# Capped experts of a two-layer block: own buffers for each expert, five gathers ahead of the first scatter, outputs signalled tile by tile

## The chip, the cores and the metric

The kernel runs on one core of a Trainium2 chip. The metric is the device time of one execution in microseconds (us), lower is better. The kernel before was timed three times: 1220.89, 1223.37 and 1225.88 us, a median of 1223.37 us.

## The reference

16 sequences of 256 tokens with 128 channels pass through two layers, each an attention and a feed-forward part, each wrapped as x + layernorm(part(...)). The first feed-forward part is a gated mixture, the second attention is a power attention. Only the last part is touched here, a mixture with capped experts (8 experts, the last of which passes its tokens through; 7 real ones, 512 tokens each, hidden width 512):

```python
cap = math.ceil(n_tok / n_exp * CAPACITY_FACTOR)               # 4096 / 8 = 512
weights_flat = softmax(x @ router_w.T + router_b)               # top 2 kept, the rest zero
sorted_indices = jnp.argsort(-expert_mask, axis=0)[:cap]        # first 512 tokens of each expert
inputs = x_flat[used_idx] * sorted_mask                         # gather
h = jax.nn.relu(jnp.einsum('ceh,ehi->cei', inputs, experts_inter))
out = jnp.einsum('cei,eih->ceh', h, experts_out) * in_w[..., None]
combined = jnp.zeros_like(x_flat).at[used_idx].add(out)         # scatter
combined = combined + x_flat * (noop_w * noop_mask)[:, None]
# then: x + layernorm(combined)
```

## The kernel before, in words

The three earlier parts (`soft_layers`, `gated_layer`, `power_layer`) and the routing (`route`) fill the span up to about 1107 us. `route` leaves in on-chip memory the row numbers for each expert's gather and scatter (`idx_in`, `idx_out`, 28 columns of 128 rows: 7 experts of 4 tiles) and in HBM the table `tokens` (all tokens, with their two weights beside the 128 channels).

Then comes `capped_mixture` (L2336 on), a program of its own on each engine, tied by semaphores. For each expert e of 7:

- GpSimd (POOL) issues `gather(e)`, four indirect DMAs (L2411) of 128 rows each from `tokens` into `xe`, and `scatter(e)`, four indirect DMAs (L2418) of 128 rows each from `res` into the HBM tensor `expert_outputs`. Only GpSimd issues these, one after the other. `gather(e)` for e of 3 and more waits until the buffer of expert e-3 is free (`s_turn`, `s_two`), `scatter(e)` until VectorE has scaled that expert's outputs (`s_res`). The loop at the end of the GpSimd program sets the order.
- TensorE (PE) transposes the four tiles (`turn`, L2446), multiplies by the first weight in 4 matmuls (`up`, L2454) and by the second in 16 (`down`, L2463). Its order is up(e), turn(e+1), down(e-1). An fp32 matmul stands in the trace as two records.
- ScalarE (ACT) evicts the transposes (L2509) and applies relu (L2514).
- VectorE (DVE) forms the slot weights from the gathered rows (`slot_weights`, L2546 and L2549), scales the four output tiles into `res` (`scale`, L2557) and multiplies five tiles of the tokens by the pass-through weight (`pass_through`, L2563).

`xe` has three buffers, `res`, `slot_w`, `xT` and `hid` two. The output tiles of one expert share one of two PSUM banks, by e % 2.

When all 28 scatters have landed (`s_sent`), SyncE (SP) loads `expert_outputs` back in 16 DMAs (L2393, `got`). TensorE adds per block of four tiles the pass-through rows (`passed`, L2485) and the two loaded halves (`gathered`, L2491); the first four blocks' `passed` come before the wait for `s_sent`, the other four behind it. VectorE, ScalarE and GpSimd normalise and add the residual (L2581, L2521, L2529, L2425), and SyncE stores each block.

Of the kernel before, what the change touches and what calls it, by code (L numbers as in the profile page):

```python
# [30 lines left out]
F32 = mybir.dt.float32  # L31
# [4 lines left out]
ALU = mybir.AluOpType  # L36
# [2299 lines left out]
def capped_mixture(nc, region, idx_in, idx_out, pick, noop, xe, Y, X, cst, cstb, wi, wo, out, yd, od):  # L2336

    NX, TB, FC = NE - 1, CAP // P, F1 // P  # L2340
    NBLK = NTILE // TB
    with ExitStack() as ctx:  # L2342
        take = semaphores(nc, ctx)
# [6 lines left out]

        xT = sb("xT", [P, 2, CAP])
        hid = sb("hid", [P, 2, FC, CAP])
        res = sb("res", [P, 2, TB, D])
        got = sb("got", [P, 2, NTILE, D])
        stats = sb("stats", [P, NTILE, 6])
        mv = sb("mv", [P, NTILE, 2])
        rs = sb("rs", [P, NTILE])
        nm = sb("nm", [P, NTILE])
        two = sb("two", [P, TB, 2])
        slot_w = sb("slot_w", [P, 2, TB])  # L2360
        lv = sb("lv", [P, TB])
        eps = sb("eps", [P, 1])
        ps = ctx.enter_context(nc.psum_tensor("cps", [P, 8, 512], F32))
        turn_ps, hid_ps, out_ps = ps[:, 0:2, :], ps[:, 2:6, :], ps[:, 6:8, :]
        s_ready = sem("s_ready")
        s_xe = [sem(f"s_xe{k}") for k in range(3)]
# [6 lines left out]
        s_sent = [sem(f"s_sent{k}") for k in range(2)]  # L2373
        s_got = [sem(f"s_got{k}") for k in range(NBLK)]
        s_pass = sem("s_pass")
        s_two = sem("s_two")
# [8 lines left out]

        @block.sync
        def _(sp):
            sp.wait_ge(s_sent[0], 16 * TB * 4)
            sp.wait_ge(s_sent[1], 16 * TB * 3)
# [12 lines left out]
        def _(pool):  # L2402
            pool.memset(eps[:], EPS_LN).then_inc(s_ready, 1)

            def gather(e):
                if e >= 3:
                    pool.wait_ge(s_turn, e - 2)
                    pool.wait_ge(s_two, 2 * (e - 3) + 1)
                for c in range(TB):
                    t = e * TB + c  # L2410
                    pool.indirect_dma_start(xe[:, e % 3, c, :], None, yd,  # L2411
                                            bass.IndirectOffsetOnAxis(ap=idx_in[:, t:t + 1], axis=0)).then_inc(s_xe[e % 3], 16)

            def scatter(e):
                pool.wait_ge(s_res, e + 1)
                for c in range(TB):
                    t = e * TB + c
                    pool.indirect_dma_start(od, bass.IndirectOffsetOnAxis(ap=idx_out[:, t:t + 1], axis=0),  # L2418
                                            res[:, e % 2, c, :], None)\
                        .then_inc(s_sent[e % 2], 16)  # L2420

            def residual(n):
                pool.wait_ge(s_f, n + 1)
                part = slice(TB * n, TB * n + TB)
# [12 lines left out]
        @block.tensor  # L2437
        def _(pe):
            ident = cst[:, C_IDENT:C_IDENT + P]

            def turn(e):
                pe.wait_ge(s_xe[e % 3], 16 * TB * (e // 3 + 1))
                if e >= 2:
                    pe.wait_ge(s_xT, e - 1)
                for c in range(TB):
                    last = pe.transpose(turn_ps[:, e % 2, c * P:(c + 1) * P], xe[:, e % 3, c, 0:D], ident)  # L2446
                last.then_inc(s_turn, 1)

            def up(e):
                pe.wait_ge(s_xT, e + 1)  # L2450
                for c in range(FC):
                    if e >= 1:
                        pe.wait_ge(s_hid, FC * (e - 1) + c + 1)
                    pe.matmul(hid_ps[:, c, :], wi[:, e, c * P:(c + 1) * P], xT[:, e % 2, :], start=True, stop=True)\  # L2454
                      .then_inc(s_hp, 1)

            def down(e):
                pe.wait_ge(s_hid, FC * (e + 1))
                if e >= 2:
                    pe.wait_ge(s_res, e - 1)  # L2460
                for t in range(TB):
                    for c in range(FC):
                        last = pe.matmul(out_ps[:, e % 2, t * D:(t + 1) * D], hid[:, e % 2, c, t * P:(t + 1) * P],  # L2463
                                         wo[:, e, c, :], start=(c == 0), stop=(c == FC - 1))
                last.then_inc(s_op, 1)
# [12 lines left out]

            def passed(n):
                if 2 <= n < 6:  # L2480
                    pe.wait_ge(s_hid, FC * (NX - 1) + n - 1)
                if n >= 6:
                    pe.wait_ge(s_res, NX - 1 if n % 2 != (NX - 1) % 2 else NX)
# [12 lines left out]
            for n in range(NBLK):  # L2496
                if n == NBLK // 2:
                    pe.wait_ge(s_sent[0], 16 * TB * 4)
                passed(n)
            for n in range(NBLK):  # L2500
                gathered(n)

        @block.scalar
        def _(act):
            for e in range(NX):
# [4 lines left out]
                for c in range(FC):  # L2510
                    act.wait_ge(s_hp, FC * e + c + 1)
                    if e >= 2:
                        act.wait_ge(s_op, e - 1)
# [26 lines left out]
        @block.vector  # L2540
        def _(dve):
            def slot_weights(e):
                dve.wait_ge(s_xe[e % 3], 16 * TB * (e // 3 + 1))
                if e >= 1:
                    dve.wait_ge(s_two, 2 * e)
                dve.tensor_tensor(two[:], xe[:, e % 3, :, D:D + 2], pick[:, TB * e:TB * e + TB, :], ALU.mult)\  # L2546
                   .then_inc(s_two, 1)
                dve.wait_ge(s_two, 2 * e + 1)
                dve.tensor_reduce(slot_w[:, e % 2, :], two[:], AX.X, ALU.add).then_inc(s_two, 1)  # L2549

            def scale(e):
                dve.wait_ge(s_op, e + 1)
                dve.wait_ge(s_two, 2 * e + 2)
                if e >= 2:
                    dve.wait_ge(s_sent[e % 2], 16 * TB * (e // 2))
                for c in range(TB):
                    last = dve.tensor_scalar(res[:, e % 2, c, :], out_ps[:, e % 2, c * D:(c + 1) * D],  # L2557
                                             slot_w[:, e % 2, c:c + 1], None, ALU.mult)
                last.then_inc(s_res, 1)

            def pass_through(e):
                for t in range(5 * e, min(NTILE, 5 * e + 5)):
# [27 lines left out]
def build(nc, dram, out):  # L2590
    with ExitStack() as ctx:
# [151 lines left out]
```

## Time and profile before

| | us |
|---|---|
| median of three runs | 1223.37 (1220.89 to 1225.88) |
| the profiled execution's own time | 1220.48 |
| its span | 1218.7 |
| mean granted TensorE clock in it | 0.969 of full speed |
| GpSimd busy in the span | 663.2 (54%) |
| TensorE busy in the span | 1113.3 (91%) |

The span is the time from the first to the last recorded instruction; 1.78 us of the execution's own time lie around it. The clock is given as a share of full speed (2.4 GHz): 1.00 is 2.4 GHz and 0.50 is 1.2 GHz. In a timeline row, the bracket at the end is the idle time of the engine before that row and what ended it; "issue" there means that the engine waited for nothing that the profile shows. A gather or scatter on GpSimd counts as busy while GpSimd issues it; the data land later.

### The profile page before, as it was taken

To read this page: it belongs to the slowest core of one execution; us is meant where nothing else is said; L and a number is where in the kernel's file an instruction comes from. 1 tells how busy PE (TensorE), PEld (TensorE's weight loads), DVE (VectorE), ACT (ScalarE), POOL (GpSimd) and SP (SyncE) were. 2 spreads that over 40 slices of the span, in tenths; PEclk is the share of its full clock that TensorE was granted. 3 is DMA by queue.
4 is the path that set the end of the run, shared out by engine and by line. 5 is a ranking of instruction groups with operands and counts; after the bars stand their busy time and mean duration, and the time that the engine had idled before them with its cause. 6 is when DMAs were issued, how large, how long until landed. Compare 5 with 4: busy or idle time off the path is not lost. (4 is left out here: it accounts for less than half of the span.)

```text
span 1218.7 us, 33462 instructions
## 1 busy us (share of the span) xinstructions
PE 1113.3 (91%) x11747; PEld 628.6 (52%) x11747; DVE 994.4 (82%) x2703; ACT 855.1 (70%) x1830; POOL 663.2 (54%) x695
## 2 busy tenths in 40 slices
PE   5999999999999998999999998999999999928976
PEld 2344444444444444666556555555566665524652
DVE  4899999999999896689988899789899999773223
ACT  1688888888888887656555555687899998733314
POOL 3234334554433330556556667577788887734753
PEclk9999999999999998999999999999899999957998
DMA  4111111111111110000000000001112222032117
GB/s 121 32 40 38 41 39 41 41 37 39 42 41 45 37 32 11 2 1 2 1 2 2 2 1 9 22 18 48 41 48 56 57 57 56 21 140 44 50 42 207
DMA packets 83460, 48.91 MB, mean 40 GB/s; under 512 B 17432, under 2 KB 80353, under 8 KB 83297
## 3 DMA queue, kind: packets, MB, share of 16 engines
q1 hardware_dynamic: 80816, 42.62, 13.5%
q0 software_dynamic: 1792, 3.70, 1.1%
q8 instruction: 97, 1.59, 0.6%
q14 instruction: 67, 0.54, 0.1%
q10 hardware_dynamic: 688, 0.46, 0.1%
HBM read 16.52 MB, written 10.26 MB: 22 GB/s over the span
## 5 line engine op out<-in xcount | busy, mean ns | idle before, releaser
L627 DVE TENSOR_REDUCE mxsS<-scoreS 128x2 f32<-128x512 f32 x512 | 328.7, 684 | 38.9 <-PE scoreS L766 33.9
L515 ACT ACTIVATE PTS<-stS 128x512 f32<-128x512 f32 x512 | 283.5, 591 | 53.0 <-PE stS L770 52.8
L2014 POOL TENSOR_TENSOR ghid<-gprod,ghid 128x512 f16<-128x512 f32 x144 | 165.8, 1159 | 139.4 <-ACT ghid L2144 138.2
L766 PE MATMUL scoreS<-QK 31*128 31x256 f16 x1024 | 172.5, 280 | 24.0 <-DVE mxsS L627 11.4
L971 POOL TENSOR_TENSOR PTP<-PTP,EP 128x512 f32<-128x512 f32 x128 | 163.2, 1285 | 50.7 <-ACT PTP L1199 50.6
L770 PE MATMUL stS<-QK 32*128 32x256 f16 x1024 | 168.7, 277 | 1.3 <-ACT PTS L515 1.3
L2144 ACT ACTIVATE ghid<-gprod 128x512 f16<-128x512 f32 x144 | 90.2, 627 | 94.4 <-DVE gprod L2303 93.5
L691 PE MATMUL pvS<-PTS,Vx 128*32 128x256 f32 x2048 | 138.8, 389 | 0.4
L1372 DVE TENSOR_SCALAR AP<-score_psP 128x768 int32<-128x768 int32 x128 | 121.5, 949 | 10.6 <-PE score_psP L1528 10.0
L766 PEld LDWEIGHTS scoreS<-QK 31*128 31x128 f16 x1024 | 53.8, 93 | 145.6 <-DVE mxsS L627 92.5
L1199 ACT ACTIVATE PTP<-AP,epsP 128x768 f32<-128x768 f32 x128 | 119.2, 931 | 6.6 <-DVE AP L1372 5.9
L388 POOL TENSOR_TENSOR rsS<-veS,halfS 128x2 f32<-128x2 f32 (+1 forms) x32 | 28.0, 874 | 172.2 <-DVE veS L595 89.2
L2096 PE MATMUL up_ps<-ghT,split 128*128 128x512 f16 x432 | 116.8, 379 | 3.3 <-DVE gprod L2303 3.3
L2091 PE MATMUL gate_ps<-ghT,split 128*128 128x512 f16 x432 | 116.9, 379 | 2.9 <-ACT gsg L2157 2.8
L2303 DVE TENSOR_TENSOR gprod<-gsg,up_ps 128x512 f32<-128x512 f32 x144 | 96.1, 682 | 23.9 <-ACT gsg L2157 18.1
L2070 PEld LDWEIGHTS down_ps<-split,ghid 128*128 128x128 f16 x1728 | 102.0, 98 | 17.6 <-issue 3.6
L2070 PE MATMUL down_ps<-split,ghid 128*128 128x128 f16 x1728 | 108.2, 219 | 0.0
L2157 ACT ACTIVATE gsg<-gate_ps 128x512 f32<-128x512 f32 x144 | 84.4, 586 | 28.0 <-PE gate_ps L2091 26.6
L1209 ACT ACTIVATE EP<-decay_psP 128x512 f32<-128x512 f32 x128 | 75.6, 591 | 20.3 <-PE decay_psP L1510 19.6
L691 PEld LDWEIGHTS pvS<-PTS,Vx 128*32 128x32 f32 x2048 | 53.8, 110 | 49.4 <-issue 21.8
L2096 PEld LDWEIGHTS up_ps<-ghT,split 128*128 128x128 f16 x432 | 41.4, 98 | 56.7 <-DVE gprod L2303 8.0
L2268 DVE SCALAR_TENSOR_TENSOR gacc<-down_ps,gcomb,gacc 128x128 f32<-128x128 f32 x224 | 62.6, 341 | 0.0
(341 smaller groups left out, 2233.6 us busy)
## 6 DMA issues: line engine op xcount, KB each, us to landing
QK<-HLS SPq DMA_DIRECT2D x384, 32.0 KB, 1.9
QK<-HLP SPq DMA_DIRECT2D x192, 32.0 KB, 1.9
expert_outputs<-tzero SPq DMA_DIRECT2D x8, 512.0 KB
cgot<-expert_outputs SPq DMA_DIRECT2D x16, 256.0 KB, 4.9
tokens<-XB SPq DMA_DIRECT2D x16, 128.0 KB, 3.1
out_dram<-X SPq DMA_DIRECT2D x8, 256.0 KB, 2.3
wi<-L_ffn_experts_inter_dram SPq DMA_DIRECT2D x7, 256.0 KB, 3.1
wo<-n_L_ffn_experts_out_dram SPq DMA_DIRECT2D x7, 256.0 KB, 3.8
```

The lines of the kernel that those rows point to most:

```text
L515: act.activation(PT[:, n % NPT, :], st_ps[:, (NS * t + n) % 3, :], ACT.Exp, scale=SCALE).then_inc(s_exp, 1)
L627: dve.tensor_reduce(mxs[:, u // 4, :, at], score_ps[:, n % 2, :].rearrange("p (c s) -> p c s", c=TC), AX.X, ALU.max).then_inc(s_max, 1)
L691: last = pe.matmul(pv_ps[32 * j:32 * j + 32, q], Vx[:, t % 3, c, 4 * g + j, :], PT[:, (4 * g + (j ^ 2)) % NPT, S * c:S * c + S], start=(c ...
L766: scored = pe.matmul(score_ps[:, k, cols], QK[part, new, g, 0, rows], QK[part, new, g, 1, :], start=True, stop=True)
L770: turned = pe.matmul(st_ps[:, (NS * t + n) % 3, cols], QK[part, old, g, 1, rows], QK[part, old, g, 0, :], start=True, stop=True)
L971: eng.tensor_tensor(w, w, E[:, n % NE, :], ALU.mult).then_inc(s_wd if n % NU in MULT_BY_DVE else s_wp, 1)
L1199: act.activation(PT[:, n % NW, :], A[:, n % NA, :], ACT.Square, bias=eps[:, 0:1]).then_inc(s_sq, 1)
L1372: dve.tensor_scalar(A[:, n % NA, :].bitcast(I32), score_ps[:, n % 2 * WU:n % 2 * WU + WU].bitcast(I32), 0x7FFFFFFF, None, ALU.bitwise_and) ...
L2014: pool.tensor_tensor(hid[:, n // FC % NHID, 1, c, :], prod[:, n % NPROD, :], hid[:, n // FC % NHID, 0, c, :], ALU.subtract).then_inc(s_hid, 1)
L2070: last = pe.matmul(down_ps[:, x % 2, t * D:(t + 1) * D], hid[:, x % NHID, lh, c, t * P:(t + 1) * P], down_w[:, lw, x % EX, c, :], start=(c ...
L2091: last = pe.matmul(gate_ps[:, n % 2, :], gate_w[:, lw, e, cols], hT[:, n // NQ % 2, lh, :], start=(k == 0), stop=(k == 2))
L2096: last = pe.matmul(up_ps[:, n % 3, :], up_w[:, lw, e, cols], hT[:, n // NQ % 2, lh, :], start=(k == 0), stop=(k == 2))
```

## The change

Every expert gets its own buffer for gathered rows (`xe`, 7 instead of 3), for outputs (`res`, 7 instead of 2) and for slot weights; to make room, the last stage may use all on-chip memory behind its start. The gathers then wait for nothing, and each has a semaphore of its own. GpSimd issues five experts' gathers first, then for each expert its scatter and after it, while there are any left, the gather of expert e+5. VectorE signals `s_res` after each tile instead of after each expert, and every single scatter waits for its own tile. TensorE signals `s_op` after each half of an expert's down matmuls. For the last expert the halves lie in different PSUM banks, so that VectorE scales the first while TensorE writes the second; the second half then waits until expert 5's tiles are scaled. For experts 0 to 5 VectorE still waits for both halves. One semaphore counts all scatters.

```diff
-    NX, TB, FC = NE - 1, CAP // P, F1 // P
+    NX, TB, FC, AHEAD = NE - 1, CAP // P, F1 // P, 5
...
-        res = sb("res", [P, 2, TB, D])
+        res = sb("res", [P, NX, TB, D])
...
+        def out_tile(e, t):
+            bank = t // 2 if e == NX - 1 else e % 2
+            return out_ps[:, bank, t * D:(t + 1) * D]
...
             def gather(e):
-                if e >= 3:
-                    pool.wait_ge(s_turn, e - 2)
-                    pool.wait_ge(s_two, 2 * (e - 3) + 1)
...
             def scatter(e):
-                pool.wait_ge(s_res, e + 1)
                 for c in range(TB):
                     t = e * TB + c
+                    pool.wait_ge(s_res, t + 1)
                     pool.indirect_dma_start(od, bass.IndirectOffsetOnAxis(ap=idx_out[:, t:t + 1], axis=0),
-                                            res[:, e % 2, c, :], None)\
-                        .then_inc(s_sent[e % 2], 16)
+                                            res[:, e, c, :], None)\
+                        .then_inc(s_sent, 16)
...
-            gather(0)
-            gather(1)
-            gather(2)
+            for e in range(AHEAD):
+                gather(e)
             for e in range(NX):
-                if e + 3 < NX:
-                    gather(e + 3)
                 scatter(e)
+                if e + AHEAD < NX:
+                    gather(e + AHEAD)
...
             def down(e):
                 pe.wait_ge(s_hid, FC * (e + 1))
...
+                for half in range(2):
+                    if half == 0 and e >= 2:
+                        pe.wait_ge(s_res, TB * (e - 1))
+                    if half == 1 and e == NX - 1:
+                        pe.wait_ge(s_res, TB * e)
+                    for t in range(2 * half, 2 * half + 2):
+                        for c in range(FC):
+                            last = pe.matmul(out_tile(e, t), hid[:, e % 2, c, t * P:(t + 1) * P],
+                                             wo[:, e, c, :], start=(c == 0), stop=(c == FC - 1))
+                    last.then_inc(s_op, 1)
...
             def scale(e):
-                dve.wait_ge(s_op, e + 1)
                 dve.wait_ge(s_two, 2 * e + 2)
-                if e >= 2:
-                    dve.wait_ge(s_sent[e % 2], 16 * TB * (e // 2))
                 for c in range(TB):
...
+                    dve.wait_ge(s_op, 2 * e + 1 + (c // 2 if e == NX - 1 else 1))
+                    dve.tensor_scalar(res[:, e, c, :], out_tile(e, c), slot_w[:, e, c:c + 1], None, ALU.mult)\
+                       .then_inc(s_res, 1)
...
-        xe = region("xe", [P, 3, CAP // P, D + 2], F32)
+        region = Region(nc, region.at, nc.sbuf_usable_end)
+        xe = region("xe", [P, NE - 1, CAP // P, D + 2], F32)
```

On GpSimd, the DMAs of the last stage stood before in this order (`xe` is a gather, `expert_outputs` a scatter, x16 are four experts):

```order
L2411 DMA xe<-tokens,idx_in 128x130 x16
L2418 DMA expert_outputs<-cres,idx_out 8320x128 x4
L2411 DMA xe<-tokens,idx_in 128x130 x4
L2418 DMA expert_outputs<-cres,idx_out 8320x128 x4
L2411 DMA xe<-tokens,idx_in 128x130 x4
L2418 DMA expert_outputs<-cres,idx_out 8320x128 x4
L2411 DMA xe<-tokens,idx_in 128x130 x4
L2418 DMA expert_outputs<-cres,idx_out 8320x128 x16
L2425 TENSOR_TENSOR X<-X,XB 128x512 x8
```

With the change the same 56 DMAs stand on GpSimd in this order:

```order
L2412 DMA xe<-tokens,idx_in 128x130 x20
L2419 DMA expert_outputs<-cres,idx_out 8320x128 x4
L2412 DMA xe<-tokens,idx_in 128x130 x4
L2419 DMA expert_outputs<-cres,idx_out 8320x128 x4
L2412 DMA xe<-tokens,idx_in 128x130 x4
L2419 DMA expert_outputs<-cres,idx_out 8320x128 x20
L2426 TENSOR_TENSOR X<-X,XB 128x512 x8
```

The gather of expert 4 has moved ahead of the first scatter, that of 5 ahead of the second and that of 6 ahead of the third.

On TensorE, the two last experts' down matmuls stood before in this way, with the `passed` matmuls behind them (a semaphore's name in the brackets is that of its first use in the program, and the number is used again: `s_one` is `s_res` here, `s_bias` is `s_hid`, `s_flat` is `s_xT` and `full_MXaS` is `s_pass`):

```order
L2463 MATMUL cps<-wo,chid 128x128 [waits s_one,s_bias]
L2463 MATMUL cps<-wo,chid 128x128 x15
L2463 MATMUL cps<-wo,chid 128x128 [waits s_one,s_bias]
L2463 MATMUL cps<-wo,chid 128x128 x15
L2485 MATMUL cps<-XB,cst 128x512 [waits full_MXaS,s_flat]
```

With the change, at the same place on TensorE (`s_set` is `s_res`, `s_spread` is `s_hid`, `s_one` is `s_xT` and `free_TS` is `s_pass`):

```order
L2466 MATMUL cps<-wo,chid 128x128 [waits s_set,s_spread]
L2466 MATMUL cps<-wo,chid 128x128 x15
L2466 MATMUL cps<-wo,chid 128x128 [waits s_set,s_spread]
L2466 MATMUL cps<-wo,chid 128x128 x7
L2466 MATMUL cps<-wo,chid 128x128 [waits s_set]
L2466 MATMUL cps<-wo,chid 128x128 x7
L2488 MATMUL cps<-XB,cst 128x512 [waits free_TS,s_one]
```

No matmul has moved; the last expert's 16 have one more wait in their middle.

## Rows read from the trace of the kernel before

**Rows 1.** The page: its head, and its share of the last chain by engine.
```profile
span 1218.7 us, 33462 instructions
...
POOL 4%; PE 2%; issue 2%; ACT 1%; DMA 0%; DVE 0%; POOLq 0%
```

**Rows 2.** The chain of waits, its last part: start us, us, what.
```profile
1175.11 1.14 DVE cres L2557 x4
...
1185.42 2.24 DMA expert_outputs<-cres,idx_out
1187.71 5.13 PE cps L2485 x8
1192.84 3.45 PE cps L2491 x8
```

**Rows 3.** Timeline of GpSimd in the last stage: start us, duration, what, idle before.
```profile
1107.88 1.23 POOL L2411 DMA_INDIRECT xe<-tokens,idx_in  x1 [0.70 <-issue]
1109.40 0.95 POOL L2411 DMA_INDIRECT xe<-tokens,idx_in  x1 [0.30 <-issue]
...
1126.90 0.94 POOL L2411 DMA_INDIRECT xe<-tokens,idx_in  x1 [0.30 <-issue]
1130.17 1.00 POOL L2418 DMA_INDIRECT expert_outputs<-cres,idx_out  x1 [2.33 <-DVE cres L2557]
...
1135.31 0.99 POOL L2411 DMA_INDIRECT xe<-tokens,idx_in  x1 [0.30 <-issue]
...
1140.37 1.00 POOL L2418 DMA_INDIRECT expert_outputs<-cres,idx_out  x1 [0.30 <-issue]
...
1145.50 0.99 POOL L2411 DMA_INDIRECT xe<-tokens,idx_in  x1 [0.30 <-issue]
...
1169.50 0.97 POOL L2418 DMA_INDIRECT expert_outputs<-cres,idx_out  x1 [3.86 <-DVE cres L2557]
...
1176.51 0.97 POOL L2418 DMA_INDIRECT expert_outputs<-cres,idx_out  x1 [2.22 <-DVE cres L2557]
...
1181.60 0.97 POOL L2418 DMA_INDIRECT expert_outputs<-cres,idx_out  x1 [0.30 <-issue]
...
1185.42 0.97 POOL L2418 DMA_INDIRECT expert_outputs<-cres,idx_out  x1 [0.30 <-issue]
```

**Rows 4.** Timeline of TensorE's matmuls in the same stage.
```profile
1128.57 3.60 PE L2454 MATMUL cps<-cxT,wi 128*128 128x512 f32 x8
...
1136.01 3.60 PE L2454 MATMUL cps<-cxT,wi 128*128 128x512 f32 x8
1141.69 0.66 PE L2446 MATMUL cps<-cst,xe 128*128 128x128 f32 x4 [2.08 <-DMA xe<-tokens,idx_in]
1142.18 5.37 PE L2463 MATMUL cps<-wo,chid 128*128 128x128 f32 x32
...
1162.20 0.66 PE L2446 MATMUL cps<-cst,xe 128*128 128x128 f32 x4 [2.60 <-DMA xe<-tokens,idx_in]
...
1171.33 7.31 PE L2463 MATMUL cps<-wo,chid 128*128 128x128 f32 x64
1180.34 3.67 PE L2485 MATMUL cps<-XB,cst 128*128 128x512 f32 x8 [1.70 <-DVE XB L2563]
```

**Rows 5.** DMA issues of the last stage: what, count, median us from issue to landing.
```profile
xe<-tokens,idx_in POOLq DMA_INDIRECT x28, 2.5
expert_outputs<-cres,idx_out POOLq DMA_INDIRECT x28, 2.2
```

**Rows 6.** Timeline of VectorE: the pass-through tiles behind expert 5's scaling.
```profile
1176.15 1.06 DVE L2563 TENSOR_SCALAR XB<-XB,noop 128x128 f32<-128x128 f32 x5
```

**Rows 7.** Engines and granted TensorE clock in two stretches of 2 us.
```profile
core 0: us, PE busy (x) PEld busy (x) DVE busy (x) ACT busy (x) POOL busy (x), PEclk, DMA share, GB/s
1144.00:1146.00 2.00, 2.00 (x11) 2.00 (x11) 0.00 (x0) 0.00 (x0) 1.47 (x2) 0.50 0.19 66
...
1188.00:1190.00 2.00, 2.00 (x3) 0.88 (x3) 0.00 (x0) 0.00 (x0) 0.00 (x0) 0.50 0.51 152
```

More of the change, by code:

```diff
@@ L2359, in capped_mixture @@
         two = sb("two", [P, TB, 2])
-        slot_w = sb("slot_w", [P, 2, TB])
+        slot_w = sb("slot_w", [P, NX, TB])
         lv = sb("lv", [P, TB])
@@ L2364, in capped_mixture @@
         turn_ps, hid_ps, out_ps = ps[:, 0:2, :], ps[:, 2:6, :], ps[:, 6:8, :]
+        def out_tile(e, t):
+            bank = t // 2 if e == NX - 1 else e % 2
+            return out_ps[:, bank, t * D:(t + 1) * D]
         s_ready = sem("s_ready")
-        s_xe = [sem(f"s_xe{k}") for k in range(3)]
+        s_xe = [sem(f"s_xe{e}") for e in range(NX)]
         s_turn = sem("s_turn")
@@ L2372, in capped_mixture @@
         s_res = sem("s_res")
-        s_sent = [sem(f"s_sent{k}") for k in range(2)]
+        s_sent = sem("s_sent")
         s_got = [sem(f"s_got{k}") for k in range(NBLK)]
@@ L2387, in _ @@
         def _(sp):
-            sp.wait_ge(s_sent[0], 16 * TB * 4)
-            sp.wait_ge(s_sent[1], 16 * TB * 3)
+            sp.wait_ge(s_sent, 16 * TB * NX)
             rows = od[0:2 * NT, :].rearrange("(c t p) d -> c p t d", c=2, p=P)
@@ L2405, in gather @@
             def gather(e):
-                if e >= 3:
-                    pool.wait_ge(s_turn, e - 2)
-                    pool.wait_ge(s_two, 2 * (e - 3) + 1)
                 for c in range(TB):
                     t = e * TB + c
-                    pool.indirect_dma_start(xe[:, e % 3, c, :], None, yd,
-                                            bass.IndirectOffsetOnAxis(ap=idx_in[:, t:t + 1], axis=0)).then_inc(s_xe[e % 3], 16)
+                    pool.indirect_dma_start(xe[:, e, c, :], None, yd,
+                                            bass.IndirectOffsetOnAxis(ap=idx_in[:, t:t + 1], axis=0)).then_inc(s_xe[e], 16)
             def scatter(e):
-                pool.wait_ge(s_res, e + 1)
                 for c in range(TB):
                     t = e * TB + c
+                    pool.wait_ge(s_res, t + 1)
                     pool.indirect_dma_start(od, bass.IndirectOffsetOnAxis(ap=idx_out[:, t:t + 1], axis=0),
-                                            res[:, e % 2, c, :], None)\
-                        .then_inc(s_sent[e % 2], 16)
+                                            res[:, e, c, :], None)\
+                        .then_inc(s_sent, 16)
             def residual(n):
@@ L2441, in turn @@
             def turn(e):
-                pe.wait_ge(s_xe[e % 3], 16 * TB * (e // 3 + 1))
+                pe.wait_ge(s_xe[e], 16 * TB)
                 if e >= 2:
@@ L2445, in turn @@
                 for c in range(TB):
-                    last = pe.transpose(turn_ps[:, e % 2, c * P:(c + 1) * P], xe[:, e % 3, c, 0:D], ident)
+                    last = pe.transpose(turn_ps[:, e % 2, c * P:(c + 1) * P], xe[:, e, c, 0:D], ident)
                 last.then_inc(s_turn, 1)
@@ L2458, in down @@
                 pe.wait_ge(s_hid, FC * (e + 1))
-                if e >= 2:
[L2460 to L2465, printed above, removed]
+                for half in range(2):
[8 more added lines that the diff above has]
+                    last.then_inc(s_op, 1)
             for _ in range(24):
@@ L2482, in passed @@
                 if n >= 6:
-                    pe.wait_ge(s_res, NX - 1 if n % 2 != (NX - 1) % 2 else NX)
+                    pe.wait_ge(s_res, TB * NX)
                 part = Y[:, TB * n:TB * n + TB, :].rearrange("p t d -> p (t d)")
@@ L2497, in _ @@
                 if n == NBLK // 2:
-                    pe.wait_ge(s_sent[0], 16 * TB * 4)
+                    pe.wait_ge(s_sent, 16 * TB * NX)
                 passed(n)
@@ L2512, in _ @@
                     if e >= 2:
-                        act.wait_ge(s_op, e - 1)
+                        act.wait_ge(s_op, 2 * (e - 1))
                     act.activation(hid[:, e % 2, c, :], hid_ps[:, c, :], ACT.Relu).then_inc(s_hid, 1)
@@ L2542, in slot_weights @@
             def slot_weights(e):
-                dve.wait_ge(s_xe[e % 3], 16 * TB * (e // 3 + 1))
+                dve.wait_ge(s_xe[e], 16 * TB)
                 if e >= 1:
                     dve.wait_ge(s_two, 2 * e)
-                dve.tensor_tensor(two[:], xe[:, e % 3, :, D:D + 2], pick[:, TB * e:TB * e + TB, :], ALU.mult)\
+                dve.tensor_tensor(two[:], xe[:, e, :, D:D + 2], pick[:, TB * e:TB * e + TB, :], ALU.mult)\
                    .then_inc(s_two, 1)
                 dve.wait_ge(s_two, 2 * e + 1)
-                dve.tensor_reduce(slot_w[:, e % 2, :], two[:], AX.X, ALU.add).then_inc(s_two, 1)
+                dve.tensor_reduce(slot_w[:, e, :], two[:], AX.X, ALU.add).then_inc(s_two, 1)
             def scale(e):
-                dve.wait_ge(s_op, e + 1)
                 dve.wait_ge(s_two, 2 * e + 2)
-                if e >= 2:
-                    dve.wait_ge(s_sent[e % 2], 16 * TB * (e // 2))
                 for c in range(TB):
-                    last = dve.tensor_scalar(res[:, e % 2, c, :], out_ps[:, e % 2, c * D:(c + 1) * D],
-                                             slot_w[:, e % 2, c:c + 1], None, ALU.mult)
-                last.then_inc(s_res, 1)
+                    dve.wait_ge(s_op, 2 * e + 1 + (c // 2 if e == NX - 1 else 1))
+                    dve.tensor_scalar(res[:, e, c, :], out_tile(e, c), slot_w[:, e, c:c + 1], None, ALU.mult)\
+                       .then_inc(s_res, 1)
             def pass_through(e):
```

## The prediction, made before the changed kernel was run

> **What bounds the kernel now.** I read the page's head and its last chain first. The span is 1218.7 us, and the chain that ended last names GpSimd before TensorE, with small shares of the whole span [rows 1]. The diff touches only the stage that starts at about 1107 us, so I asked which wait ends last there. The chain of waits, read backwards from the output, goes through the normalisation to the adding matmuls (L2491), to eight passed matmuls (L2485, 5.13 us), and from there at 1187.71 us to the landing of the last scatter, which GpSimd issued at 1185.42 us [rows 2]. Everything behind 1187.69 us hangs on that one scatter: 1218.7 - 1187.7 = 31.0 us of tail. So the question is when GpSimd issues its last scatter.
>
> GpSimd's timeline shows a nearly closed row of DMA issues [rows 3]. A gather costs 0.95 us plus a gap of 0.30: from the second to the sixteenth it is (1126.90 - 1109.40) / 14 = 1.25 us each. A group of four scatters takes 5.13 us (1140.37 to 1145.50) ahead of a gather and 5.09 us (1176.51 to 1181.60) ahead of another scatter; four gathers behind a scatter take 5.06 us (1135.31 to 1140.37). The 56 issues stretch from 1107.88 to 1185.42 us. Three gaps are longer than 0.30 us: 2.33 before the first scatter (expert 0), 3.86 before the one at 1169.50 (expert 4) and 2.22 before the one at 1176.51 (expert 5); expert 6's group begins at 1181.60 without a wait [rows 3]. Beyond the usual 0.30 they hold 2.03 + 3.56 + 1.92 = 7.51 us in which GpSimd waited for VectorE's scaled outputs. That is all that GpSimd loses.
>
> Why it waited is seen on TensorE [rows 4]. An expert takes 7.44 us there when nothing is late (up starts at 1128.57 and at 1136.01). But the transposes of experts 4 and 6 started 2.08 and 2.60 us late for their gathers, and in the down matmuls behind them the clock is at 0.50, 1.2 GHz [rows 7], so that they take 5.37 us; the hot price is 7.31 / 2 = 3.66 us [rows 4]. The gathers were late because each stood behind a scatter that had waited for the outputs of an earlier expert. It is a ring: GpSimd waits for TensorE's outputs, TensorE then for GpSimd's gathers.
>
> **The change part by part.** All sums are made against the profiled execution (span 1218.7, own time 1220.48).
>
> 1. Gathers ahead. Expert 4's four gathers go into the hole before the first scatter. The twenty gathers' last starts at 1126.90 + 4 x 1.25 = 1131.90, the first scatter at 1133.15, where before it was 1130.17: 3.0 us later, and nobody waits for it, since the loads need all 28. From there on, if no output is late: scatter 0 at 1133.15, gather 5 at 1138.28, scatter 1 at 1143.34, gather 6 at 1148.47, scatter 2 at 1153.53, then 5.09 each: 1158.6, 1163.7, 1168.8, and expert 6's at 1173.9. The last of its four starts 3.82 later (1185.42 - 1181.60 [rows 3]): 1177.7. That is 7.7 us before 1185.42.
>
> 2. Are the outputs ready by then? Gathers land 2.5 us after their issue [rows 5]. Expert 4's have landed at 1134.4, before TensorE wants them at about 1139.4; expert 5's at 1144.6, wanted at 1146.9; expert 6's last is issued at 1152.3 and lands at 1154.8, wanted at about 1154.3, so TensorE waits some 0.5 us. Up starts at 1136.01 as before, then at 1143.45, 1150.89 and 1158.8 (expert 6); down of 5 and 6 runs from 1162.3 to 1169.6 (7.31). VectorE needs 1.14 us for four tiles [rows 2]. Outputs against scatters: expert 4 about 1160.2 against 1163.7, expert 5 about 1167.1 against 1168.8, expert 6 about 1170.5 against 1173.9. The narrowest margin is 1.7 us, so GpSimd runs closed to its end. What is late next is GpSimd's own row of 56 issues.
>
> 3. Signals for each tile. GpSimd's scatters now carry 28 waits instead of 7, and the gathers lose theirs. Behind each waiting DMA the whole rest of the row is queued, and behind its end the loads and the tail. The row shows what a satisfied wait costs: the scatter at 1140.37 has one and stands behind a gap of 0.30 like those without, at 1.00 us instead of 0.97 [rows 3]. Below I bound it by 0, above by 0.40: the gap before the first gather, right behind another kind of instruction, is 0.70. I take 0.00 to 0.03 for each of 21, and 0.1 us in all, since the difference of 0.03 is also seen on a gather (0.99 at 1135.31) and so is not the wait's. VectorE's and TensorE's added signals and waits lie beside their engines' idle time.
>
> 4. The last expert in halves. Its second half's wait for expert 5's scaling falls to about 1166.0 + 1.3 = 1167.3, while the first half runs until 1166.0 + 1.8 = 1167.8: hidden by 0.5 us, and if the cover went, it would cost only TensorE time that has 3 us of margin to the scatter. The gain is nothing as well: the outputs are finished before GpSimd can send them.
>
> 5. Own buffers for outputs and slot weights. No wait before ended with a buffer's release (the three long ones ended with the scaling), so they free nothing, except that gathers may run ahead at all. Cost nothing.
>
> 6. The tail. Passed for the first four blocks starts right after the last pass-through tiles, at about 1171, and ends at 1174.7 (3.67 us [rows 4]); TensorE then waits until 1177.7 + 2.3 = 1180.0, 5.3 us, where before it waited 1187.71 - 1184.01 = 3.7 us. Behind the 3.7 us the clock was at 0.50 [rows 7], and eight matmuls took 5.13 instead of 3.67 us. At most all eight run at 1.2 GHz: 2 x 3.67 = 7.3, 2.2 us more than now; at least they take what they take hot, 1.5 less, of which the loads, then the next in line, leave perhaps 0.2. The stretches behind 2.08 and 2.60 us of idle time cost 5.37 - 3.66 = 1.7 each, 0.25 more than the 1.46 here, so I take 0.4 us.
>
> The Trainium skill, page "TensorE: Matmul & The Clock Gate", section "HAM oscillation — how this bites in real kernels", says that a wait for a DMA between two bursts drops the clock, so that the next burst starts cold. The trace agrees: 0.50 after the wait of 3.7 us. By that rule the longer wait of the changed kernel gives a cold start again and term 6 stays within 0 to 2.2 us; a reading of the trace alone gives the same bounds.
>
> Sum: -7.7 + 0.1 + 0.4 = -7.2 us. Span 1211.5, own time 1213.3. The profiled execution lies 2.9 us below the median of the runs shown; carried over, the median becomes 1223.4 - 7.2 = 1216.2, rounded 1216.
>
> **The rivals.**
> A. As above, GpSimd closed: 1216 (chance 0.72).
> B. TensorE falls behind and GpSimd waits again. For it: TensorE still waits 0.5 us for expert 6's gather, and waits of 2 us brought 1.2 GHz. Against: 0.5 us is short, and even two cold downs (3.4 us) leave expert 5's outputs at 1170.5 against 1168.8, 1.7 us lost. Time 1218 (0.10).
> C. The tail gives it back: all eight passed matmuls at 1.2 GHz, 1.8 us more than taken: 1218 (0.10).
> D. Slower: the price of waits on GpSimd. Each scatter's wait costs, in place of nothing, up to the 0.40 us that the gap of 0.70 has over 0.30. 21 x 0.40 = 8.4 us, 8.3 above my term: 1224.5. It decides from 7.3 / 21 = 0.35 us for each on. Against it stands the scatter with a satisfied wait and a gap of 0.30. Chance 0.04, and some of it lies above 0.5% only if a wait costs over 0.6 us.
> E. Nothing comes of it: GpSimd's issues stretch when they run closed beside VectorE. For each of the seven pass-through groups, 1.06 us [rows 6], an issue would be held up: about 6.8 us with the short last one, and 1223. Against it: the scatter at 1176.51 took 0.97 us in the middle of such a group (1176.15 to 1177.21), as did that at 1185.42 with VectorE idle. Chance 0.04, with everything else that could leave the time as it was. The Trainium skill, page "SBUF — State Buffer", section "SBUF: two separate sides", has such a rule: while VectorE runs an instruction that takes both ports, GpSimd cannot write the descriptors of its DMAs. The two rows just named show no trace of it.
>
> **How the numbers follow.** About 0.5% (6.1 us) is what a measurement of this kernel can tell from no change; that line is at 1217.3, only 1.3 us above my forecast, and the three runs of before lie 5 us apart. Of A some seven tenths fall below it, of B and C a third: 0.52 + 0.07, and a little for a larger gain, 0.60. Slower by over 0.5%: 0.03. The rest, 0.37, is within. For the range I take A with 4 us for the runs' own spread, and let it reach over B and C: 1211.5 to 1221.
>
> **What the changed profile would show.** Steps 1 and 2 are right if GpSimd's timeline has no gap above 0.30 us between its first gather and its last scatter, and that scatter starts at 1177 to 1179 us; wrong if a scatter waits for VectorE. TensorE should have no transpose waiting more than 1 us and no down group above 4 us. Step 3 is right if scatters with waits keep 0.97 to 1.00 us and gaps of 0.30. Step 4 is right if the last expert's first scatter doesn't wait. Step 6 shows in the passed matmuls behind the wait: 5.1 us if I neither gain nor lose, 7 for C. The prediction fails if the last scatter comes at 1182 us or later, or if the tail from its landing to the end is over 33 us.

## The result, and the profile after

| | before | with the change |
|---|---|---|
| median, runs on the same chip, us | 1224.84 (20 runs) | 1215.34 (20 runs, 1211.39 to 1222.06) |
| ratio | | 0.9929, 95% interval 0.9913 to 0.9945 |
| profiled execution: own time, span | 1220.48, 1218.7 | 1217.18, 1215.4 |
| W: first gather's start to last scatter's start | 77.54 | 70.11 |
| tail: last scatter's landing to the end | 31.0 | 32.1 |

The timeline of GpSimd in the changed kernel, first gather to last scatter, columns as in [rows 3]:

```profile
1110.92 1.23 POOL L2412 DMA_INDIRECT xe<-tokens,idx_in  x1 [0.70 <-issue]
...
1136.17 1.00 POOL L2419 DMA_INDIRECT expert_outputs<-cres,idx_out  x1 [0.30 <-issue]
...
1140.03 0.97 POOL L2419 DMA_INDIRECT expert_outputs<-cres,idx_out  x1 [0.30 <-DVE cres L2558]
...
1170.68 1.08 POOL L2419 DMA_INDIRECT expert_outputs<-cres,idx_out  x1 [0.30 <-DVE cres L2558]
1172.07 0.97 POOL L2419 DMA_INDIRECT expert_outputs<-cres,idx_out  x1 [0.30 <-DVE cres L2558]
...
1177.21 0.97 POOL L2419 DMA_INDIRECT expert_outputs<-cres,idx_out  x1 [0.30 <-issue]
...
1181.03 0.97 POOL L2419 DMA_INDIRECT expert_outputs<-cres,idx_out  x1 [0.30 <-issue]
```

The gaps of 2.33, 3.86 and 2.22 us of [rows 3] are gone. Where VectorE is still named as the releaser, the gap is the usual 0.30 us, so nothing was waited for. The last scatter starts 70.11 us after the first gather.

TensorE's matmuls in the changed kernel answer to [rows 4]:

```profile
1142.45 0.60 PE L2446 MATMUL cps<-cst,xe 128*128 128x128 f32 x4
1142.89 3.74 PE L2466 MATMUL cps<-wo,chid 128*128 128x128 f32 x32
...
1157.86 0.66 PE L2446 MATMUL cps<-cst,xe 128*128 128x128 f32 x4 [0.36 <-DMA xe<-tokens,idx_in]
1158.36 3.74 PE L2466 MATMUL cps<-wo,chid 128*128 128x128 f32 x32
...
1165.37 7.31 PE L2466 MATMUL cps<-wo,chid 128*128 128x128 f32 x64
1173.86 3.67 PE L2488 MATMUL cps<-XB,cst 128*128 128x512 f32 x8 [1.19 <-DVE XB L2563]
1183.33 5.22 PE L2488 MATMUL cps<-XB,cst 128*128 128x512 f32 x8 [5.80 <-DMA expert_outputs<-cres,idx_out]
```

The transposes of experts 4 and 6 wait 0 and 0.36 us instead of 2.08 and 2.60, and no down group is above 3.74 us. The wait for the scatters has grown from 3.70 to 5.80 us, and the eight matmuls behind it are as cold as before: 5.22 us. The granted clock there, answering to [rows 7]:

```profile
1182.00:1184.00 2.00, 0.68 (x1) 0.50 (x2) 0.00 (x0) 0.00 (x0) 0.00 (x1) 0.50 0.10 33
1184.00:1186.00 2.00, 2.00 (x3) 0.67 (x2) 0.00 (x0) 0.00 (x0) 0.00 (x0) 0.50 0.71 211
```

The chain of waits of the changed kernel ends in another way than [rows 2]:

```profile
1181.03 2.25 DMA expert_outputs<-cres,idx_out
1183.30 0.37 SPq L2397
...
1187.66 6.43 DMA cgot<-expert_outputs
1194.13 2.00 PE cps L2494 x4
1196.15 0.89 DVE cstats L2581 x4
```

It no longer goes through the cold passed matmuls but through SyncE's row of load issues, from 1183.30 on, and the landing of the load issued at 1187.66. With it the fourth block is there, 10.83 us after the scatters have landed.

### The profile page after: what moved, and what is told of

It reads as the page before. It is cut to its first block and busy times, and to the rows that moved or that the text cites. A ratio compares the mean times of both kernels' runs of the same rounds, so it can differ in the third digit from the quotient of the medians.

```text
span 1215.4 us, 33457 instructions
## 1 busy us (share of the span) xinstructions
PE 1111.4 (91%) x11747; PEld 625.7 (51%) x11747; DVE 997.1 (82%) x2703; ACT 855.4 (70%) x1830; POOL 663.5 (55%) x695
## 5 line engine op out<-in xcount | busy, mean ns | idle before, releaser
L627 DVE TENSOR_REDUCE mxsS<-scoreS 128x2 f32<-128x512 f32 x512 | 328.8, 685 | 38.1 <-PE scoreS L766 33.0
L1372 DVE TENSOR_SCALAR AP<-score_psP 128x768 int32<-128x768 int32 x128 | 121.6, 950 | 11.6 <-PE score_psP L1528 10.7
L1209 ACT ACTIVATE EP<-decay_psP 128x512 f32<-128x512 f32 x128 | 75.7, 591 | 21.7 <-PE decay_psP L1510 21.2
```

The lines of the kernel that those rows point to most:

```text
L627: dve.tensor_reduce(mxs[:, u // 4, :, at], score_ps[:, n % 2, :].rearrange("p (c s) -> p c s", c=TC), AX.X, ALU.max).then_inc(s_max, 1)
L1372: dve.tensor_scalar(A[:, n % NA, :].bitcast(I32), score_ps[:, n % 2 * WU:n % 2 * WU + WU].bitcast(I32), 0x7FFFFFFF, None, ALU.bitwise_and) ...
```

## The experiments

The same program doesn't run alike on every chip, and this came to decide what the experiments could show. So the pairs of exact copies come first, then the variants. Each chip was used in one sitting only, so wherever the text says "on chip 2", the traces can't tell the chip from the occasion.

| run | chip | gathers in a row at the start | up 0 to up 3, us | W, us | tail, us | ratio to before there | before's median there |
|---|---|---|---|---|---|---|---|
| before | not noted | 16 | 20.0 | 77.54 | 31.0 | | 1224.8 |
| the change | not noted | 20 | 20.1 | 70.11 | 32.1 | 0.9929 | 1224.8 |
| before2 | 1 | 16 | 19.9 | 77.51 | 31.3 | 1.0009 | 1223.3 |
| after2 | 1 | 20 | 19.9 | 70.02 | 32.6 | 0.9931 | 1223.3 |
| after3 | 12 | 20 | 19.9 | 69.96 | 32.3 | 0.9955 | 1220.9 |
| order_only_c | 12 | 20 | 19.9 | 69.94 | 32.2 | 0.9940 | 1220.9 |
| ahead4 | 2 | 16 | 22.5 | 81.55 | 32.5 | 0.9986 | 1230.0 |
| order_only | 2 | 20 | 28.9 | 83.25 | 31.6 | 1.0003 | 1230.0 |
| warm | 2 | 20 | 29.0 | 81.72 | 31.0 | 0.9967 | 1230.0 |
| ahead7 | 2 | 28 | 38.1 | 85.40 | 31.6 | 1.0006 | 1230.0 |
| ahead4_b | 15 | 16 | 23.3 | 81.70 | 32.3 | 0.9964 | 1230.4 |
| order_only_b | 15 | 20 | 29.3 | 83.52 | 31.1 | 1.0006 | 1230.4 |
| early_queues | 15 | 20 | 29.7 | 82.12 | 31.8 | 0.9983 | 1230.4 |
| fewer | 15 | 24 | 32.2 | 81.45 | 32.1 | | 1230.4 |

W is the difference of two starts in GpSimd's timeline, as in 1181.03 - 1110.92 = 70.11. "Up 0 to up 3" is the time on TensorE from the start of expert 0's up matmuls to that of expert 3's, as in 1139.02 - 1118.88 = 20.1; what it has above 20 us is time lost to the stalls named issue (TensorE stands still although it waits for nothing that the profile shows), with the cold matmuls behind them.

**Exact copies.** No edit.

> The changed kernel once more, word for word, beside its variants' conditions. In the first four experiments every variant showed something that neither trace of before nor of the change has: from the 28th matmul record of the first expert's down group on, TensorE stood still up to 2.6 us before single instructions, named issue, 1 to 15 us in all. Theory S (the stalls in TensorE's supply of instructions belong to the conditions of the run, not to the variants): this trace shows them too, W (first gather's start to last scatter's) is 75 to 85 us instead of 70.1, and the time is at 1226 to 1230 us. Theory V (the variants' own order or layout brings them): this trace shows none, W is 70.1 us and the ratio to the kernel before is 0.993 as measured before.

> The kernel before once more, word for word, under the same conditions as the changed kernel beside it. Theory S: stalls named issue in the first expert's down group here too, W 78 to 90 us instead of 77.5. Theory V: no stalls, W 77.5 us.

Neither copy stalled. Ratio of after2 0.9931 (0.9908 to 0.9954), W 70.02 against 77.51. That looked like theory V, but the kernel before was at 1223.3 us here and at 1230 us on chips 2 and 15, and that is no variant. The last pair was chosen to tell it apart:

> The changed kernel word for word a third time. All eight traces of variants so far (chips 2 and 15, where the kernel before had a median of 1230 us) have TensorE standing still before single instructions in the first expert's down group; the two traces of the changed kernel and the two of before (chip 1 and the first sessions, before at 1223 to 1225 us) have none. Theory S (it goes with the chip or the session): where the kernel before is at about 1230 us again, this kernel stalls too, W 78 to 86 us and 1224 to 1228 us; where before is at 1224 us, no stall, W 70.1 us and 1215 us. Theory V (it goes with the variants): never a stall here.

> The order alone a third time, in the same conditions as the changed kernel beside it. Where no stall occurs: theory of order W 70 to 71 us and the same time as the changed kernel; rival (signals, halves, own output buffers carry part) W 72 us or more. Where the stalls occur: W 82 to 84 us and a time 2 to 4 us above the changed kernel, because the scatters of an expert then start only behind its fourth scaled tile. By theory V this variant stalls even if the changed kernel beside it does not.

On chip 12 (before 1220.9 us) neither stalled. The variant that had stalled on chips 2 and 15 did not stall here, so the stalls don't belong to the variant: theory V is out. Ratios 0.9955 (0.9935 to 0.9976) and 0.9940 (0.9912 to 0.9967), the same.

**The order alone** (order_only, three times):

```diff
-        s_xe = [sem(f"s_xe{k}") for k in range(3)]
+        s_xe = [sem(f"s_xe{k}") for k in range(NX)]
...
             def gather(e):
-                if e >= 3:
-                    pool.wait_ge(s_turn, e - 2)
-                    pool.wait_ge(s_two, 2 * (e - 3) + 1)
...
-            gather(0)
-            gather(1)
-            gather(2)
+            for e in range(5):
+                gather(e)
             for e in range(NX):
-                if e + 3 < NX:
-                    gather(e + 3)
                 scatter(e)
+                if e + 5 < NX:
+                    gather(e + 5)
...
-        xe = region("xe", [P, 3, CAP // P, D + 2], F32)
+        region = Region(nc, region.at, nc.sbuf_usable_end)
+        xe = region("xe", [P, NE - 1, CAP // P, D + 2], F32)
```

> The kernel before with the order alone changed: seven buffers for gathered rows, gathers without waits, five experts' gathers ahead; still two output buffers, one signal for each expert (7 waits on GpSimd's scatters instead of 28) and no halves. Theory: W 70 to 71 us, the same time as the changed kernel within the measurement. Rival 1 (signals, halves or own output buffers carry part of the gain): W 72 us or more, because a scaling waits for the scatters of two experts earlier or a scatter for its fourth tile. Rival 2 (28 waits on GpSimd cost time each): W shorter than with the change, by 21 times the price of a wait; at 0.1 us each 68.0 us.

> The order alone, without the signals for each tile, the halves and the seven output buffers, once more for the same reason. Theory of order: no wait over 0.5 us on GpSimd, W 70 to 71 us, ratio to before 0.993. Rival 1: a scaling waits for older scatters, W 72 us or more. Rival 2 (a wait has a price): W 68 us.

Where nothing stalled, the order, with the seven buffers for gathered rows that it needs, gives the whole gain. GpSimd's row in order_only_c:

```profile
1113.86 1.23 POOL L2408 DMA_INDIRECT xe<-tokens,idx_in  x1 [0.70 <-issue]
...
1183.80 0.97 POOL L2415 DMA_INDIRECT expert_outputs<-cres,idx_out  x1 [0.30 <-issue]
```

69.94 us, against 69.96 for the whole change beside it. The signals for each tile, the halves and the five more output buffers together brought nothing there, and 28 waits cost no more than 7 (0.02 us in all). The order of before with seven gather buffers is in ahead4 alone, on chips with stalls, so the two are not cleanly separated by a run; but in the kernel before no gather on GpSimd stood behind more than its usual gap of 0.30 us, so no gather had waited for a buffer. On chips 2 and 15 W was 83.3 and 83.5 us, 1.5 and 1.4 us more than in the kernels with signals, halves and output buffers there that have five experts ahead too (warm and early_queues below). So where outputs are late these parts are worth something.

**Four ahead** (ahead4, twice; the output buffers, signals and halves of the change stay):

```diff
-    NX, TB, FC, AHEAD = NE - 1, CAP // P, F1 // P, 5
+    NX, TB, FC, AHEAD = NE - 1, CAP // P, F1 // P, 4
```

> The changed kernel with four instead of five experts' gathers ahead of the first scatter: GpSimd's order is then that of the kernel before, while the own buffers, the signals for each tile and the last expert in halves stay. I measure W, the time from the start of GpSimd's first gather to the start of its last scatter (77.5 us before, 70.1 us with the change). Theory (the order of gathers and scatters made the gain): the waits for VectorE come back at the first scatter and at experts 4 and 5, shortened by 0.8 us each time since a scatter may start behind one scaled tile instead of four; W 75 to 77 us, and 5 to 6 us slower than the changed kernel. Rival (signals and buffers made it): W stays at 70 to 72 us and the time within 2 us of the changed kernel.

> Four gathers ahead instead of five, once more, since the first try ran where TensorE's instructions came late (stalls named issue) on a chip that the changed kernel was not timed on. Without such stalls the theory of order expects: GpSimd waits for VectorE again before the first scatter (1.5 us beyond the gap of 0.30), and at experts 4 and 5; W (first gather's start to last scatter's) 75 to 77 us, time 5 to 6 us above the changed kernel, ratio to before 0.998. Rival (signals and buffers): W 70 to 72, ratio 0.993.

Ratios 0.9986 (0.9969 to 1.0002) and 0.9964 (0.9930 to 0.9998). Both ran on chips with stalls, so W (81.6, 81.7) can't be compared with the 75 to 77 expected, and how much the signals would save with four ahead is not measured. But the ring of the prediction, GpSimd waiting for outputs and TensorE then for gathers, is there. TensorE in ahead4:

```profile
1145.72 0.66 PE L2446 MATMUL cps<-cst,xe 128*128 128x128 f32 x4 [1.15 <-DMA xe<-tokens,idx_in]
...
1157.90 1.12 PE L2446 MATMUL cps<-cst,xe 128*128 128x128 f32 x4 [4.51 <-DMA xe<-tokens,idx_in]
...
1168.50 0.27 PE L2446 MATMUL cps<-cst,xe 128*128 128x128 f32 x1 [0.81 <-DMA xe<-tokens,idx_in]
```

TensorE had lost 2.5 us to the stall, and then waits 1.15 + 4.51 + 0.81 = 6.5 us for gathers, since each late output made a scatter late and it the gather behind it. With five or more ahead no transpose waited for a gather on those chips, although the stalls took 9 to 18 us.

**Seven ahead** (the same line with 7), and what the stalls are made of.

> The changed kernel with all seven experts' gathers ahead of the first scatter. Theory (with five ahead GpSimd's 56 issues are closed, and their sum is the bound): the first scatter comes 10.1 us later, W stays 70.1 us within 0.3 us, since every output is ready early, the 0.36 us wait of TensorE for expert 6's gather goes, and nothing is gained in the time. Rival (TensorE's rest of waiting for gathers still costs, or a later first scatter costs): W changes by more than 0.5 us.

W 85.4 us, ratio 1.0006 (0.9989 to 1.0023), on chip 2: my expectation of an unchanged W was missed, for a reason that I had not thought of. TensorE in ahead7:

```profile
1124.62 3.18 PE L2466 MATMUL cps<-wo,chid 128*128 128x128 f32 x27
1128.93 0.35 PE L2466 MATMUL cps<-wo,chid 128*128 128x128 f32 x1 [1.14 <-issue]
1130.33 0.27 PE L2466 MATMUL cps<-wo,chid 128*128 128x128 f32 x1 [1.05 <-issue]
1133.15 0.37 PE L2466 MATMUL cps<-wo,chid 128*128 128x128 f32 x1 [2.56 <-issue]
...
1142.96 1.01 PE L2454 MATMUL cps<-cxT,wi 128*128 128x512 f32 x1 [1.79 <-issue]
1145.06 4.85 PE L2454 MATMUL cps<-cxT,wi 128*128 128x512 f32 x6 [1.09 <-issue]
```

Single matmuls, which in the down group have no wait of their own behind the first, start 1.4 to 2.8 us apart. It ends at 1145 us; GpSimd's 28 gathers in a row end at 1142.5. In all eight traces with stalls, the longer the first row of gathers, the more time is lost: 2.5 and 3.3 us with 16, 8.9 to 9.7 us with 20, 12.2 us with 24 and 18.1 us with 28. Within some 3 us of the row's end this stall is over, in ahead4 and ahead4_b too, where GpSimd then sits idle for 4 us. In six of the eight traces (not in ahead7 and fewer) a smaller one comes later in the stage, 1.2 to 3.2 us of idle time in all. In order_only its largest part lies 4 us and more behind the last gather, which ends at 1166.2, while GpSimd scatters or waits:

```profile
1170.59 0.51 PE L2459 MATMUL cps<-wo,chid 128*128 128x128 f32 x3 [0.47 <-issue]
1172.01 0.27 PE L2459 MATMUL cps<-wo,chid 128*128 128x128 f32 x1 [0.91 <-issue]
1173.41 2.39 PE L2459 MATMUL cps<-wo,chid 128*128 128x128 f32 x20 [1.13 <-issue]
```

So TensorE's instructions come late mostly while GpSimd gathers, on chips 2 and 15, and not on the others. What makes them late no trace shows: that the gathers do it is argued from the time and the length of the large stall, and the small ones don't fit it everywhere.

**TensorE kept busy in the tail** (warm):

```diff
                 if n == NBLK // 2:
+                    pe.wait_ge(s_res, TB * NX)
+                    for _ in range(20):
+                        pe.matmul(ps[:, 7, :], cstb[:, 0:P], cstb[:, P:2 * P].unsqueeze(1).to_broadcast([P, 4, P]),
+                                  start=True, stop=True)
                     pe.wait_ge(s_sent, 16 * TB * NX)
```

> The changed kernel with 20 added bf16 matmuls of 512 columns into a PSUM bank that is overwritten later, placed on TensorE between the fourth and the fifth block's passed matmuls, ahead of its wait for the scatters (they compute nothing that is used). They should fill some 4.3 of the 5.8 us of TensorE's wait and keep the clock at 2.4 GHz. If the clock in the tail costs what I took (0.4 us and the 1.5 us of the kernel before), the passed matmuls behind the wait take 3.7 instead of 5.2 us and the tail from the last scatter's landing to the end goes from 32.1 to 31 us or less. Rival (the loaded rows bound the tail, not TensorE): passed take 3.7 us, the first loaded block is then waited for, and the tail is unchanged within 0.3 us.

```profile
1192.57 4.48 PE L2503 MATMUL cps<-cstb 128*128 128x512 bf16 x20
1196.88 3.60 PE L2488 MATMUL cps<-XB,cst 128*128 128x512 f32 x8
1200.42 1.98 PE L2494 MATMUL cps<-cgot,cst 128*128 128x512 f32 x4
1203.15 12.64 PE L2494 MATMUL cps<-cgot,cst 128*128 128x512 f32 x28 [0.75 <-DMA cgot<-expert_outputs]
```

The passed matmuls take 3.60 us at the full clock, the second block is then waited for, and the tail is 31.0 us, 1.1 to 1.6 less than in the three traces of the changed kernel. That meets the first expectation, but it doesn't show that the clock did it: order_only and order_only_b, with cold passed matmuls (5.40 us) on such chips, have tails of 31.6 and 31.1 us, and ahead7, where they ran at the full clock without any help (3.70 us, behind a wait of 3.59), has 31.6. Ratio 0.9967 (0.9949 to 0.9984) on chip 2. This kernel holds the whole change, so it also bounds what the change is worth there: with the added matmuls 0.2 to 0.5%.

**Tail rearranged** (early_queues):

```diff
-                if n == NBLK // 2:
+                if n == NBLK - 1:
+                    pe.wait_ge(s_res, TB * NX)
+                    for _ in range(8):
...
+            act.wait_ge(s_sent, 16 * TB * NX)
+            halves = od[0:2 * NT, :].rearrange("(c t p) d -> c p t d", c=2, p=P)
+            for n in range(NBLK):
+                act.dma_start(got[:, 1, n * TB:(n + 1) * TB, :], halves[1, :, n * TB:(n + 1) * TB, :])\
+                   .then_inc(s_got[n], 16)
```

> The changed kernel with two changes in the tail: seven of the eight blocks' passed matmuls ahead of the wait for the scatters with 8 added unused bf16 matmuls behind them, so that only the last block's stands behind the wait; and the sixteen loads of the scattered rows issued half from SyncE and half from ScalarE. If TensorE's five us of passed matmuls behind the landing hold up the first block, and the sixteen issues of 0.5 to 0.8 us on one queue the later ones, the tail from the landing to the end (32.1 us) falls by 1 to 3 us. Rival (the bytes of the loads bound the tail: 4 MB at about 300 GB/s are 14 us, and each block's normalisation 1.8 us): the tail stays within 0.5 us, since the fourth block still lands 10.5 us after the start.

```profile
1193.72 1.02 PE L2487 MATMUL cps<-XB,cst 128*128 128x512 f32 x2
1197.32 15.70 PE L2493 MATMUL cps<-cgot,cst 128*128 128x512 f32 x32 [2.58 <-DMA cgot<-expert_outputs]
```

TensorE is ready 2.58 us before the first block has landed; the tail is 31.8 us, and the ratio 0.9983 (0.9958 to 1.0007) on chip 15. Nothing is gained, as the rival had it, but not for its reason that the bytes of the loads bound the tail. The chain of waits of early_queues:

```profile
1193.20 4.08 DMA cgot<-expert_outputs
1197.32 5.41 PE cps L2493 x8
1202.76 0.89 DVE cstats L2589 x4
...
1203.96 0.31 ACT clv L2527
```

The first load is waited for, TensorE's next eight matmuls are cold behind that wait (5.41 us; the granted clock is 0.71 from 1197 to 1201), and from the second block on, at 1203.96, ScalarE (L2527, L2529, L2535) runs closed for the 21.0 us to the end, some 1.8 us for each block. The kernel before has the same row, from 1197.52 on, 21.2 us before its end; the changed kernel has it too, with one more wait inside (point 6 below). So the loads, and a cold start behind them, set when ScalarE's row starts; the row itself is the larger part of the tail, and neither of the two edits shortens it.

**Four scatters less** (fewer):

```diff
-            sp.wait_ge(s_sent, 16 * TB * NX)
+            sp.wait_ge(s_sent, 16 * TB * (NX - 1))
...
-                scatter(e)
+                if e > 0:
+                    scatter(e)
...
-                    pe.wait_ge(s_sent, 16 * TB * NX)
+                    pe.wait_ge(s_sent, 16 * TB * (NX - 1))
```

> The changed kernel without expert 0's four scatters (its outputs never reach the sum; 52 instead of 56 issues on GpSimd). If GpSimd's closed row is the bound and nothing stands close behind it, W falls by four scatters, 5.1 us, to 65.0. By my table of outputs against scatters something does: expert 5's first tile is scaled 58.3 us after the first gather's start (trace of the changed kernel, less 0.36 us of TensorE's wait that goes with the earlier gather), while its scatter would be due at 57.0. So I expect one gap of about 1.6 us before expert 5's first scatter and W at 66 to 67 us, 3 to 4 us less. Rival (TensorE is already the bound): W falls by less than 1 us.

Inconclusive. Without the first scatters the gathers of six experts, 24, stood in one row:

```profile
1143.17 0.94 POOL L2412 DMA_INDIRECT xe<-tokens,idx_in  x1 [0.30 <-issue]
1155.53 1.00 POOL L2419 DMA_INDIRECT expert_outputs<-cres,idx_out  x1 [11.42 <-DVE cres L2559]
```

This was on chip 15: TensorE lost 12.2 us, GpSimd waited 11.42 us before its first scatter, and W was 81.5 us. What stands behind GpSimd's closed row is not measured.

## Why the prediction was right

Forecast 1216, measured 1215.34 us. How near the two levels lie is in part luck. The forecast took 7.2 us off a median of 1223.37 us for three runs of the kernel before; over 20 runs that median is 1224.84 us, and the ratio makes the change worth 8.7 us. Its mechanism, the gaps in GpSimd's row, was right. Point by point:

1. The gap sum. Forecast: the three waits go, 7.7 us earlier. Measured: W from 77.54 to 70.11, 7.4 us. The closed row is 70.1 where I had 1177.7 - 1107.88 = 69.8. In order_only_c it is the order that does it. Right.
2. Outputs ready in time. The narrowest margin was to be 1.7 us at expert 5; VectorE began to scale its tiles at 1169.21 and needed 1.13 us, and its first scatter went at 1172.07 with a gap of 0.30: again 1.7 us, and expert 6's gather was waited for 0.36 us against my 0.5. Right.
3. Waits on GpSimd. Forecast 0.1 us in all. 28 waits against 7 on one chip: 69.96 against 69.94 us. The slower rival, 0.40 us each, is refuted.
4. The halves bring and cost nothing: right, as far as that pair tells, which tests them together with the rest; and TensorE's two last down groups stand in one row of 7.31 us without a gap, as before.
5. Buffers for outputs: nothing, by the same pair. The prediction had them free because no wait had ended with their release.
6. The tail. I took 0.4 us more and bounded it by 2.2; it is 32.1 to 32.6 us in three traces against 31.0 and 31.3 in two of before, 0.8 to 1.6 more. The mis-sized term. The cold matmuls are a small part, 5.22 to 5.55 us in the three against 5.13 and 5.21. What I had not priced is that the fourth block's loads land 10.83 us after the scatters (11.3 and 12.0 in the copies) where before TensorE had them at 10.34. ScalarE's row of normalisations, closed before from the second block on, then waits once more. ScalarE in the changed kernel:

```profile
1197.35 0.30 ACT L2524 ACTIVATE clv<-cmv,ceps 128x4 f32<-128x4 f32 x1 [0.38 <-DVE cmv L2584]
1198.37 1.51 ACT L2532 ACTIVATE XB<-cps,cnm,crs 128x128 f32<-128x128 f32 x4 [0.48 <-DVE cnm L2575]
```

These are 0.86 us (1.20 and 0.86 in the copies, none in either trace of before), most of the excess. Why the loads come later is open. The clock is not the reason, for the loads don't pass through TensorE. SyncE's row of sixteen load issues is itself longer: 13.43 us against 12.93, and 14.47 and 13.87 in the copies against 13.00.

Together the stage gives 7.4 - 1.1 = 6.3 us: from the first gather to the end 104.5 to 104.9 us in three traces against 110.8 and 111.0 in two, a little less than the 7.2 forecast. The ratios of the three measurements, -8.7, -8.4 and -5.5 us, lie around it; the first one's interval (6.7 to 10.7 us) begins just above, and no trace says where the 2.4 us between 6.3 and 8.7 come from. The stage starts at 1107.9 to 1119.2 us in the five traces of the two kernels, so the code ahead of it, which is the same, moves the time by more than the change does, and one profile of each would not have told: their spans differ by only 3.3 us.

The rival that the gain is given back was not true in those three measurements, where the kernel before is at 1221 to 1225 us. On chips 2 and 15 it largely is, by a mechanism that the prediction didn't have: the kernels closest to the change (warm and early_queues) gained 0.3 and 0.2%, the latter not clear of nothing, and the order alone nothing. With five experts' gathers in a row TensorE loses 6 us more than with four, and this takes most of the 7.4 us. The kernel before is 5 to 10 us slower there than elsewhere, which fits a stall of some 3 us in it as well and the ring behind it; but neither it nor the changed kernel itself was profiled there, so that part is argued, not shown.

## What to carry to other kernels

When one engine issues both the transfers that feed a pipeline and those that drain it, put the feeding ones so far ahead that no feed stands behind a drain that can wait: the wait otherwise goes round in a ring and comes back. The gain is at most the sum of the gaps in the issuing engine's row, less what the engines behind it give back, and the new bound is its closed row, so count its issues before refining signals and buffers that nobody waits for. Try an order on more than one chip before choosing how far ahead.

## What was not expected of the hardware

- On chips 2 and 15 TensorE got its instructions late while GpSimd issued gathers in a row (up to 2.6 us ahead of one matmul, 18.1 us in all), most of it where the program has no wait. The loss in the first stall follows the number of gathers in the row; smaller stalls came later in six of the eight traces. On chip 12 the order alone, which had stalled on chips 2 and 15, had none, nor had any trace of the kernel before or the changed one. What the two share is not shown by the traces.
- GpSimd's issues beside VectorE's pass-through scaling: at 1170.68 one took 1.08 instead of 0.97 us, the longest of the 28 scatters. So what the prediction's rival E feared costs at most 0.11 us for one issue here; the 28 scatters together took 0.26 us more than 0.97 us each.
- The passed matmuls behind the wait for the scatters were at 1.2 GHz in the kernel before (5.13 us behind 3.70 us of idle time) and at 2.4 GHz in ahead7 (3.70 us behind 3.59).
- No version that beats the changed kernel was found on a chip without stalls; warm, the only candidate, was timed only where they occur.
